# A two-layer decoder on one Trainium2 core: the first expert layer computed on tiles of sorted rows instead of by all experts for all tokens

## What is computed

```python
probs = softmax(xf @ w_router)
top_vals, top_idx = top_k(probs, 2)
gates = top_vals / sum(top_vals)
cw = einsum('tk,tke->te', gates, one_hot(top_idx, 8))
h1 = einsum('td,edh->eth', xf, w1)
h3 = einsum('td,edh->eth', xf, w3)
y = einsum('eth,ehd->etd', silu(h1) * h3, w2)
out = einsum('etd,te->td', y, cw)
out = out + silu(xf @ sw1) * (xf @ sw3) @ sw2
```

## Time and profile before

| | |
|---|---|
| median of 3 runs | 922.12 us (919.76 to 922.5) |
| the profiled execution | 927.22 us |
| its span, first to last instruction | 925.2 us |
| TensorE, VectorE, ScalarE, GpSimd busy | 802.7, 758.9, 516.5, 502.1 us |
| mean granted TensorE clock | 0.969 of full |

### The profile page before, as it was taken

How to read it: one execution, slowest core, us unless ns; L and a number is a source line. 1 busy time by engine, 2 the same in 40 slices (tenths; PEclk the granted TensorE clock), 3 DMA queues, 4 the chain that set the end, 5 groups by cost and what they waited for, 6 DMA issues and landing times.

```text
span 925.2 us, 14908 instructions
## 1 busy us (share of the span) xinstructions
PE 802.7 (87%) x5193; PEld 592.3 (64%) x5193; DVE 758.9 (82%) x1384; ACT 516.5 (56%) x954; POOL 502.1 (54%) x501
## 2 busy tenths in 40 slices
PE   9977777777798999999998789998989998999881
PEld 7463232323266888888886567786766677888771
DVE  7479999999987489999889967786998979667663
ACT  5867666666638535555375132226665592088771
POOL 6669999999952022132149923546444300177773
PEclk9979999999999899999999989999999999999996
DMA  7000000000000031233000000000000040296554
GB/s 210 0 1 0 0 1 0 1 0 1 1 1 0 13 115 64 66 123 94 16 1 1 0 1 1 1 1 1 2 25 2 26 115 24 52 151 160 154 131 159
DMA packets 36741, 39.68 MB, mean 43 GB/s; under 512 B 5132, under 2 KB 28698, under 8 KB 35899
## 3 DMA queue, kind: packets, MB, share of 16 engines
q1 hardware_dynamic: 34170, 33.62, 11.9%
q0 software_dynamic: 2496, 5.12, 3.6%
HBM read 30.86 MB, written 7.86 MB: 42 GB/s over the span
## 4 chain that ended last, share of the span: by engine, by line
PE 34%; DVE 16%; POOL 12%; issue 6%; ACT 5%; DMA 2%; POOLq 0%; DVEq 0%; SPq 0%; ACTq 0%
PE ps L1820 9%; PE ps L2017 3%; POOL y_rows L664 3%; PE ps L1813 3%; PE ps L2194 2%; PE ps L2249 2%; POOL G L659 2%; DVE small L1589 2%; PE ps L2384 1%; POOL R L574 1%; PE ps L1893 1%; DVE R L1550 1%; PE ps L2239 1%; DVE G L1592 1%; POOL R L575 1%
## 5 line engine op out<-in xcount | busy, mean ns | idle before, releaser
L1820 PE MATMUL ps<-xhl,whl 128*128 128x512 f32 x576 | 143.8, 398 | 2.9 <-ACT G L874 1.8
L1820 PEld LDWEIGHTS ps<-xhl,whl 128*128 128x128 f32 x576 | 107.7, 190 | 27.7 <-issue 3.3
L1254 DVE TENSOR_TENSOR_SCAN R<-ps,R 128x1024 f32<-128x1024 f32 x43 | 97.7, 2279 | 10.4 <-POOL R L498 5.9
L489 POOL TENSOR_TENSOR R<-G,R 128x1024 f32<-128x1024 f32 x43 | 100.7, 2356 | 8.4 <-ACT R L735 4.3
L794 ACT ACTIVATE ps<-G,negAb,negA 128x508 f32<-128x508 f32 x128 | 95.0, 779 | 0.5 <-DVE R L1254 0.5
L1872 PE MATMUL ps<-bc,sel 96*128 96x512 bf16 x128 | 46.1, 387 | 47.3 <-ACT LN L742 23.0
L1893 PE MATMUL ps<-R,ident 128*128 128x512 f32 x172 | 82.0, 599 | 0.2 <-POOL R L498 0.2
L1872 PEld LDWEIGHTS ps<-bc,sel 96*128 96x128 bf16 x128 | 12.5, 98 | 98.7 <-ACT LN L742 36.0
L874 ACT ACTIVATE G<-ps 128x512 f32<-128x512 f32 x72 | 42.8, 599 | 58.4 <-PE ps L1820 56.7
L735 ACT COPY R<-ps 128x512 f32<-128x512 f32 x64 | 37.5, 586 | 66.3 <-PE ps L1872 66.3
L659 POOL DMA_INDIRECT G<-xn_rows,token x39 | 39.4, 1009 | 59.1 <-DVE per_tile L1752 45.8
(11 more groups left out here) (383 smaller groups left out, 2140.9 us busy)
## 6 DMA issues: line engine op xcount, KB each, us to landing
R<-in_exp_wi_dram SPq DMA_DIRECT2D x39, 256.0 KB, 3.8
G<-cw_by_expert SPq DMA_DIRECT2D x6, 1024.0 KB, 4.6
ew<-in_w_dram SPq DMA_DIRECT2D x24, 128.0 KB, 2.2
y_rows<-zeros SPq DMA_DIRECT2D x1, 2048.0 KB, 9.0
xn_rows<-LN SPq DMA_DIRECT2D x8, 256.0 KB
G<-in_exp_wo_dram SPq DMA_DIRECT2D x8, 256.0 KB, 4.8
G<-y_rows SPq DMA_DIRECT2D x4, 512.0 KB, 5.6
X<-in_x_dram SPq DMA_DIRECT2D x4, 256.0 KB, 3.2
```

The source lines that it names most:

```text
L489: gp.tensor_tensor(halves(dBu[i % 3]), duT[:, :, gcols(i // NS)], Bsb[:, i % 4:i % 4 + 1, :].broadcast_to([P, HI, GT]), ALU.mult).then_inc ...
L1254: v.tensor_tensor_scan(hst[i % 3], bank(2 * j, 2).rearrange("p h n -> p (h n)"), dBu[i % 3], 0.0, ALU.mult, ALU.add).then_inc(S["scanned"], 1)
L1820: ins = mm(mix(out) if n == N_WIN1 else out, whl[:, wslot(n), i, m * P:(m + 1) * P], rhs, start=k == 0, stop=k == 2)
```

## The change

The 8 routed experts of the first layer are no longer computed for all tokens. As in the second layer, the 4096 pairs are placed in 39 tiles of 128 rows. Here the tokens' normalised rows, with the row's target number and its weight behind the 128 features (130 numbers, `RW`), are written to a DRAM buffer `rows_by_expert` at their place: 32 indirect transfers of 128 rows by GpSimd (`send_rows`). In this buffer every expert has 2048 rows, so that a group's rows can be placed before the later groups are counted; SyncE clears it early in the program. Then, for each tile, SyncE reads a first row and an expert's number, loads the 128 rows (one transfer, 65 KB) and the expert's `w1` and `w3` (two transfers, 128 KB each); TensorE transposes the rows and computes the up products in plain fp32 (4 of 128x128x128), reads the expert's number into a register of its own and takes the down weights (2 products) from `w2` of all experts, which is loaded once. GpSimd scatters each tile's result to `first_y_rows`; when all 39 have landed SyncE loads them back in 4 transfers of 512 KB, and VectorE adds two rows to each token. The shared expert is computed first, after the routing of all four groups, and no longer beside the others. The number of tiles is a constant of the program.

```diff
@@ SyncE
-            for k in range(E + 1):
-                if k >= 2:
-                    sp.wait_ge(S["down0"], NG * (k - 1))
...
+            sp.wait_ge(S["blank"], 1)
+            for first in range(0, ROWS, N):
+                n = min(N, ROWS - first)
+                sp.dma_start(row_dram[first:first + n].rearrange("(r p) c -> p r c", p=P), blank[:].unsqueeze(1).broadcast_to([P, n // P, RW]))\
+                    .then_inc(S["blank"], 16)
...
+            sp.wait_ge(S["plan1"], 1)
+            sp.wait_ge(S["xs_sent"], 16 * 2 * B)
+            sp.wait_ge(S["up_mm"], M0 * NG)
+            for i in range(NT):
+                first = sp.value_load(token[0:1, i:i + 1], min_val=0, max_val=E * N + 6 * P)
+                if i >= 4:
+                    wait(sp, f"xl{i % 4}", 16 * (i // 4))
+                sp.dma_start(row_at(i), row_dram[bass.ds(first, P), :]).then_inc(S[f"xl{i % 4}"], 16)
+                e = sp.value_load(tile_e[0:1, i:i + 1], min_val=0, max_val=E - 1)
+                if i >= 4:
+                    wait(sp, "e_up", i - 3)
+                for part, name in enumerate(("w1", "w3")):
+                    sp.dma_start(w13_now[:, i % 4, part * M0 * P:(part + 1) * M0 * P], a[name][bass.ds(e, 1), :, :].rearrange("e p n -> (e p) n"))\
+                        .then_inc(S[f"ew{i % 4}"], 16)
+            sp.wait_ge(S["y1_sent"], 16 * NT)
+            for g in range(NG):
+                sp.dma_start(y1_in(g).rearrange("p b k d -> p b (k d)"),
...
@@ GpSimd
+            ln_scale(2, range(NG - 1))
+            wait(pool, "blank_in", 16 * (E + 1))
+            send_rows(0, (0,))
+            ln_scale(2, (NG - 1,))
+            send_rows(0, range(1, GB))
+            for g in range(1, NG):
+                send_rows(g)
+            for i in range(NT):
+                wait(pool, "e_y", i + 1)
+                gp.indirect_dma_start(y1_dram[:, :], bass.IndirectOffsetOnAxis(ap=goes_to[:, i:i + 1], axis=0), y1_at(i), None)\
+                    .then_inc(S["y1_sent"], 16)
@@ VectorE
+            route_shift(2)
+            ln_lower(2, 1)
+            route_choose(2)
+            route_place(2)
...
+            for s in range(NT + 3):
+                i = s - 2
+                if 0 <= i < NT:
+                    wait(dve, "e_silu", i + 1)
...
+                    v.tensor_tensor(eh_at(i), es_at(i), bank(2 + i % 2)[:, 0, M0 * P:], ALU.mult).then_inc(S["e_hid"], 1)
...
+            for g in range(NG):
+                wait(dve, f"y1_in{g}", 16)
+                step(v.tensor_tensor(X[:, gb(g), :], X[:, gb(g), :], y1_in(g)[:, :, 0], ALU.add))
+                step(v.tensor_tensor(X[:, gb(g), :], X[:, gb(g), :], y1_in(g)[:, :, 1], ALU.add))
+                ln_stats(3, g)
+                if g:
+                    ln_norm(3, g - 1)
@@ TensorE
+            unread(7, 60)
+            pe.wait_ge(S["plan1"], 1)
+            pe.wait_ge(S["res0"], NG)
+            wait(pe, "ew_in", 16 * E)
+            for s in range(NT + 3):
+                if s < NT:
+                    wait(pe, f"xl{s % 4}", 16 * (s // 4 + 1))
+                    if s >= 2:
+                        wait(pe, "e_xt", s - 1)
+                    nc.tensor.transpose(bank(s % 2)[:, 0, 0:P], row_at(s)[:, 0:D], ident[:]).then_inc(S["e_t_mm"], 1)
+                i = s - 1
+                if 0 <= i < NT:
+                    wait(pe, "e_xt", i + 1)
+                    wait(pe, f"ew{i % 4}", 32 * (i // 4 + 1))
...
+                        ins = mm(bank(2 + i % 2)[:, 0, m * P:(m + 1) * P], w13_now[:, i % 4, m * P:(m + 1) * P], ext_at(i), start=True, stop=True)
+                    ins.then_inc(S["e_up"], 1)
+                i = s - 3
+                if i >= 0:
+                    e = pe.value_load(tile_e[0:1, i:i + 1], min_val=0, max_val=E - 1)
+                    wait(pe, "e_hid", i + 1)
...
+                        ins = mm(bank(4 + i % 2)[:, 0, 0:D], eh_at(i)[:, m * P:(m + 1) * P], w2[:, bass.ds(e * (M0 * D) + m * D, D)],
+                                 start=m == 0, stop=m == M0 - 1)
```

More of the change, by code:

```diff
@@ L1332, in _, with hidden @@
             ln_lower(2, 1)
-            ln_norm(2, 3)
+            route_choose(2)
+            route_place(2)
+            route_shift(3)
+            ln_lower(2, 2)
+            route_choose(3)
+            route_place(3)
+            ln_lower(2, 3)
+            def hidden(i):
+                if i >= 2:
+                    dve.wait_ge(S["down0"], i - 1)
+                for m in range(M0):
+                    dve.wait_ge(S["silu0"], M0 * i + m + 1)
+                    v.tensor_tensor(hidr[:, i % 2, m * GT:(m + 1) * GT], sh[:, i % 2, m * GT:(m + 1) * GT],
+                                    bank(6 + m)[:, 0, :], ALU.mult).then_inc(S["hid0"], 1)
@@ new lines, in _ @@
+            v.tensor_scalar(tile_e[:], per_tile[:, 0], float(E - 1), None, ALU.min)
+            step(v.tensor_tensor(skipped, ended, per_e[:, 2].unsqueeze(1).broadcast_to([P, NT, E]), ALU.mult))
+            step(v.tensor_reduce(per_tile[:, 1], skipped, AX.X, ALU.add))
+            v.tensor_tensor(token[:], per_tile[:, 1], tile_at[:], ALU.add).then_inc(S["plan1"], 1)
+            hidden(0)
+            hidden(1)
+            add_shared(0)
+            hidden(2)
+            add_shared(1)
+            hidden(3)
@@ L2012, in down_T, with shared_down @@
+            router_logits(1)
+            transpose_xn(2, 2)
+            places(1)
+            transpose_xn(2, 3)
+            router_logits(2)
+            places(2)
+            router_logits(3)
+            places(3)
+            def shared_down(c):
+                pe.wait_ge(S["hid0"], M0 * (c + 1))
                 if c >= 2:
                     pe.wait_ge(S["res0"], c - 1)
[L2014 to L2018 removed]
@@ new lines, in _ @@
+            shared_down(NG - 1)
+            pe.wait_ge(S["w_lru"], 16 * 6)
+            for k in range(HI):
+                ins = nc.tensor.transpose(bank(7)[:, 0, k * P:(k + 1) * P], w["Win1"][:, k, :], ident[:])
+            ins.then_inc(S["wt1_mm"], 1)
+            wait(pe, "wt1_ev", 1)
+            for j, name in enumerate(("Wv", "Wl")):
+                for k in range(HI):
+                    ins = mm(bank(6)[:, 0, j * DI:(j + 1) * DI], Win1T[:, k, :], w[name][:, k, :], start=k == 0, stop=k == HI - 1)
@@ L2084, in _ @@
+            unread(7, 40)
+            for g in range(NG):
+                transpose_xn(3, g, between=3)
+                if g < NG - 1:
+                    unread(7, 12)
             pe.wait_ge(S["w_lru"], 16 * 6)
```

496 lines of the change are left out of this document (228 added, 268 removed).

## The result

The changed kernel takes 959.07 us (median of 3 runs, 958.13 to 959.75), against 922.12: ratio 1.040, 95% interval 1.037 to 1.043. It is slower, as forecast, by 37 us and not 20. Its profiled execution has a span of 957.3 us, 32.1 above the 925.2 before. TensorE is still the fullest engine but is busy 783.9 us, only 18.8 us less than before, although some 145 us of expert products are gone: the tiles' own products (about 65 us in 100), 133 more unread ones (all of them take 85.3 us on the page, 53.4 before) and the routing's counting products at half clock took most of it back.

The account below looks back on a forecast made before the run. TensorE's dense expert work bounded the old stage; SyncE's issuing would bound the new tiles. Routing, shared expert, unread products, tiles and tail put the next block at 486.5 instead of 466.2, 20 us later: 942 us, range 928 to 960.

Parts of the forecast that it names:

- What bounds the tiles: Tile loop: SyncE's two register loads and three issues set the pace, 2.71 us per tile, 92.1 us for 34 tiles.
- The unread products: Ahead of the tiles: 60 unread products take 14 us, executed whether or not there is something to wait for.
- Routing, "35 us": Routing ahead of the shared expert: VectorE's list decides, 35 us, so the last lower half of norm 2 ends at 325.
- A wait of 0 to 2.4, in sum 4.4: Routing: VectorE waits after each choice for TensorE's counting products, 6 to 13 of 0.28 us each; 4.4 us in sum.
- The 40 unread products there only fill this wait: Tail, before the next block: the 40 unread products only fill the wait for loads back and norm 3, adding nothing.
- The rival of half clock: Tiles: TensorE at 1.2 GHz, 3.1 to 3.8 us per tile, ending 15 to 40 us later, 957 to 982; chance 0.11.
- Rows at 366 us: Rival at the tiles' start: row transfers take 2 us, not 1.31, rows there at 366; 15 us more, 957; chance 0.07.
- SyncE's gaps are not paid: Rival in the tiles: half the gaps gone gives 925 us, all gone 914, 28 us less; chance 0.11, 0.08 faster.
- Clearing the buffer: Early in the program: the 9 MB that clear the row buffer cost nothing, since the DMA engines are idle then.
- The median: Profiled execution before was 5.1 us above the runs' median; 20 us more on the median 922.1 gives 942 us.
- at most 42: Upper bound on the routing's time, given as 30 to 42 us.
- at most 24: Upper bound on the tail's time before the next block, given as 16 to 24 us.

Follow-up runs that it names:

- e2: Changed kernel with each tile's gate and up weights fetched in one transfer instead of two: 941.40 us, ratio 1.0185 to the kernel before.
- e4: Changed kernel with one more register load per tile on SyncE (three instead of two): 976.49 us, ratio 1.056 to the kernel before.
- e3: Changed kernel without TensorE's register load, every tile using the first expert's down weights: 956.44 us, ratio 1.034 to the kernel before.
- e5: Changed kernel with row loads issued from ScalarE's list, twelve tiles ahead, instead of SyncE's: 922.23 us, ratio 0.998 to the kernel before.
- e12: Changed kernel without the 60 unread products, one weight transfer per tile, row loads split SyncE/ScalarE, 65 fitted unread products in routing's waits: 901.17 us, ratio 0.978.
- e6: Changed kernel with 104 unread products put into TensorE's waits in the routing: 959.88 us, ratio 1.039 to the kernel before.
- e7: Changed kernel without the unread products inside and behind norm 3's group transposes, the 40 ahead kept: 961.60 us, ratio 1.0405 to the kernel before.
- e8: Changed kernel with the edits of e1, e2, e5, e6 and e7 together: 915.83 us, ratio 0.990 to the kernel before.
- e1: Changed kernel without the 60 unread products ahead of the tile loop: 953.37 us, ratio 1.029 to the kernel before.
- e9: Changed kernel with 70 unread products in the routing's waits: 996.27 us, ratio 1.047 to the kernel before, in an hour with pauses.
- e11: Changed kernel without 60 unread products, one weight transfer, row loads split SyncE/ScalarE, 70 unread products in routing, tail counts 52 and 5: 948.30 us, ratio 0.997.

## Why the prediction was right, and what was mis-sized

The forecast's chain against the trace of the changed kernel, in us of its span:

| point | forecast | trace | late, in sum |
|---|---|---|---|
| last lower half of norm 2, shared expert may start | 325 | 332.2 | 7.2 |
| shared expert done | 346 | 353.1 | 7.1 |
| folded weights done | 349 | 355.8 | 6.8 |
| 60 unread products done | 363 | 369.2 | 6.2 |
| last weights issued | 457.5 | 466.1 | 8.6 |
| last down product's end | 463.3 less 0.4 | 472.5 | 9.6 |
| first load back landed | 470 | 480.6 | 10.6 |
| next block | 486.5 | 501.3 | 14.8 |

- **What bounds the tiles** was right, and shown from both sides: an issue less is 0.55 us per tile less (e2), a register load more 0.51 more (e4), TensorE's own load changes next to nothing (e3), and with the row loads on ScalarE the stage drops to TensorE's pace (e5). The pace was 2.79, and 2.68 in the first four tiles, for 2.71. The 34 tiles of 0.08 are 2.7 us; where they come from isn't shown.
- **The unread products** take 13.4 us (14 forecast), and that they run whether or not anything waits was right. Taking them out gave 6 us by the spans and 10 by the ratios, as SyncE's list then sets the end.
- **Routing, "35 us"** is the first mis-sized term: 42.1. "A wait of 0 to 2.4, in sum 4.4" for the counting products is where it failed: the four waits are 0.94, 2.74, 3.17 and 5.41, 12.3 us and so 7.9 more. Two waits for the logits, 1.07 and 0.78, weren't in the sum at all; the other terms together came out 2.6 us lower. I had priced a counting product at full clock (0.28 each), and TensorE ran at 1.2 GHz, where eight records take 1.85 us instead of 1.06. e12 puts 5.1 us of the 7.1 down to it, by holding most of the clock; e6 alone, with the clock held but TensorE overfilled, would have said that the clock doesn't matter.
- **"The 40 unread products there only fill this wait"** is the second: it looked at the 40 and overlooked the 12 and 3 of each group, which delay the last transposes by 4 us (norm done at 496.0, transposes at 500.3). e7 and e8 show that the kernel doesn't gain when they are left out.
- **The rival of half clock** was looked for in the tiles, where the clock stayed at 1.00, and came in the routing. The Trainium skill ("TensorE: Matmul & The Clock Gate", section "HAM oscillation — how this bites in real kernels") describes a loop that computes for some 2 us and then waits 3 to 5 us for data. The tiles are no such case: their waits are 2.4 us at most, and the clock stayed at 1.00, though in e1, e3 and e4 it was 0.97, 0.98 and 0.93 over the tiles. In the routing the waits of 4 to 5 us are like that example's, and the clock was at 0.50 through them, but they are not what took it away: it fell at 290 us, behind waits of 1.04 us at most. The kernel before lost the clock at the same place (0.66 from 290 to 295 us) and had it back from 295 to 300 (1.00), with up products in the place of the waits; from 305 to 315 it was at 0.76 and 0.56 once more, with TensorE busy throughout. So what takes the clock away there stays open.
- **Rows at 366 us** as the start: no. GpSimd's transfers started every 1.26 us, the last at 340.9, and landed 2.3 us after that.
- **SyncE's gaps are not paid**: no, 2.68 with nothing to wait for. But the rival's other half, what happens when they are relieved, was worth more than it said: e5 is 39 us and not 28, since TensorE's tile is 1.45 us with the register load hidden, and not 1.9.
- **Clearing the buffer** cost nothing, as counted: the third group's statistics end at 290.1 us and at 290.5 before.
- **The median**: 37 us above that of before, the spans only 32.1, because the profiled execution of before was 5.1 above its median and that of the changed kernel was the median itself. The forecast of 942 lay 17 us under the result: 14.8 us of the chain and these 5.1, less the 3 that the rest of the program gives back.
- **How much of it was luck.** The mechanism was right, but that 959 falls within 928 to 960 is in part luck. The routing took 42.1 us for at most 42, and the tail, from the load back's issue to the next block, 475.97 to 501.30, took 25.3 for at most 24. Both bounds were passed at once, and the rest of the program's 3 us kept the sum inside.

## What to carry to other kernels

When dense work is swapped for gathered tiles, count per tile what the issuing engine's list holds (here 0.34 us an issue, 0.5 us a register load, gaps: 1.10 a pair) beside what the computing engine needs; divide the issues over engines with free time until the computing engine is the slowest, and watch that a burst of them doesn't stand ahead of that engine's own work. A stage that becomes serial and thin can run at half of TensorE's clock (0.50 from 290 to 335 us here), so price its small products at 1.2 GHz too. If a wait is filled with unread products, cut them to end with the wait: 104 products won nothing (e6), 65 fitted ones 5 us (e12). The two runs with 70 (e9, e11) won nothing either, in an hour with pauses, so this rests on one run.

## What the runs showed of the hardware that I had not expected

- A `value_load` on SyncE costs 0.51 us in the list, of which its load is 0.27 (e4). On TensorE, with the pipeline full, no time for it can be seen: in e5 the 13 records of a tile stand 0.11 us apart with it. No run has that pace without it.
- ScalarE issues such a transfer in 0.35 us, as SyncE does in 0.34 (e5, e4).
- Eight records of counting products of 32 columns take 1.85 us at half clock and 1.06 at full (changed kernel, e6). With TensorE busy for 24 of 40 us in the routing the clock stayed at 0.50; with 65 of 100 us in the tiles it stayed at 1.00, and with 64 of 100 in e4's it was 0.93.
- The kernel before took 924 us in one hour and 951 in another on the same chip. The traces of the second hour (e9 to e11) have pauses of 1 to 4 us among small instructions of TensorE and VectorE; only ratios from one hour are compared.
